# Dynamic time warping on a lane grid: from one direction in 16 segments of 100 rows to both directions in 8 segments of 188 rows

## The reference

```python
def _dtw_cost(D):                    # D: 1500 x 56 distances
    R[i, j] = D[i, j] + min(R[i-1, j], R[i, j-1], R[i-1, j-1])
def _backtrack(R, T1, T2):           # from (1499, 55) back to (0, 0)
    choice = argmin([R[i-1, j-1], R[i-1, j], R[i, j-1]])   # first minimum wins
expanded[j] += context[i]            # for each cell (i, j) of the path
x = x + tanh(g_xattn[0]) * expanded  # tokens are layer-normed before D
```

## Time and profile before

| | |
|---|---|
| median of 3 runs | 528.3 us (528.27 to 529.79) |
| profiled execution | 530.62 us, its span 528.8 us |
| TensorE, VectorE, ScalarE, GpSimd busy | 431.2, 377.7, 262.5, 86.8 us |
| mean granted TensorE clock | 0.948 |

### The profile page before, as it was taken

One profiled execution on the slowest core, in us unless ns is written; L12 is line 12 of the kernel. 1 busy time (PEld: TensorE's weight loads), 2 busy tenths in 40 slices (PEclk: granted clock), 3 DMA queues, 4 the chain that ended last, 5 costly groups with the idle time before them and its releaser, 6 DMA issues.

```text
span 528.8 us, 10186 instructions
## 1 busy us (share of the span) xinstructions
PE 431.2 (82%) x4021; PEld 254.3 (48%) x4021; DVE 377.7 (71%) x995; ACT 262.5 (50%) x454; POOL 86.8 (16%) x101
## 2 busy tenths in 40 slices
PE   9997778758888887101778899999999999989996
PEld 7444333326655573000334456666666666544444
DVE  8668999998666786865685888988979883371112
ACT  4565888655322691100102456666656567634443
POOL 1000000001000005787980000210210211100000
PEclk9999999898999999655798999999999999999999
DMA  8600674325513005963180004384384491000000
GB/s 285 226 0 23 183 213 137 109 89 152 149 58 91 28 2 126 231 150 87 36 175 1 0 1 106 74 176 103 77 177 94 84 285 37 2 1 0 0 1 17
DMA packets 28719, 50.06 MB, mean 95 GB/s; under 512 B 2464, under 2 KB 18400, under 8 KB 28672
## 3 DMA queue, kind: packets, MB, share of 16 engines
q1 hardware_dynamic: 26848, 45.74, 32.3%
q0 software_dynamic: 1536, 3.67, 2.7%
q10 hardware_dynamic: 288, 0.00, 0.0%
HBM read 39.96 MB, written 9.45 MB: 93 GB/s over the span
## 4 chain that ended last, share of the span: by engine, by line
PE 46%; DVE 35%; issue 8%; POOL 7%; ACT 3%; DMA 1%; DVEq 0%; POOLq 0%
PE banks L1626 7%; PE banks L1602 7%; POOL arena L548 6%; PE banks L1657 5%; DVE arena L1230 4%; DVE work L1259 4%; PE banks L1704 4%; DVE mx L1033 4%; PE banks L1718 4%; DVE arena L1283 2%; DVE mx L1041 2%; PE banks L1470 2%; PE banks L1316 2%; DVE work L1225 2%; PE banks L1320 2%
## 5 line engine op out<-in xcount | busy, mean ns | idle before, releaser
L1033 DVE TENSOR_REDUCE mx<-banks 112x1 f32<-112x500 f32 x168 | 106.9, 676 | 18.2 <-PE banks L1602 18.2
L778 ACT ACTIVATE arena<-banks 128x896 f32<-128x896 f32 x96 | 87.9, 917 | 49.9 <-PE banks L1657 49.2
L1340 PE MATMUL banks<-steps,one 128*128 128x500 f16 (+1 forms) x201 | 56.5, 376 | 33.8 <-DVE hcol L981 33.8
L1626 PE MATMUL banks<-arena 128*32 128x112 f32 (+1 forms) x1536 | 58.1, 265 | 3.4 <-issue 2.5
L1602 PE MATMUL banks<-ctxT,arena 128*112 128x500 bf16 x144 | 54.7, 393 | 3.7 <-DVE mx L1041 1.1
L1626 PEld LDWEIGHTS banks<-arena 128*32 128x32 f32 (+1 forms) x1536 | 33.9, 109 | 23.7 <-issue 21.0
L1340 PEld LDWEIGHTS banks<-steps,one 128*128 128x128 f16 x201 | 20.3, 103 | 48.7 <-issue 38.2
L1259 DVE SCALAR_TENSOR_TENSOR work<-twice,banks,arena 128x202 f32<-128x202 f32 x68 | 29.5, 434 | 18.8 <-PE banks L1470 18.8
L1657 PEld LDWEIGHTS banks<-arena,ctxT 128*128 128x128 bf16 (+1 forms) x576 | 37.3, 104 | 9.7 <-issue 1.9
L1657 PE MATMUL banks<-arena,ctxT 128*128 128x112 bf16 (+1 forms) x576 | 40.9, 213 | 0.0
L548 POOL DMA_INDIRECT arena<-in_w_tab,idx x32 | 34.6, 1082 | 11.6 <-issue 9.5
(11 more groups left out here) (264 smaller groups left out, 773.1 us busy)
## 6 DMA issues: line engine op xcount, KB each, us to landing
ctxT<-key_parts SPq DMA_DIRECT2D x36, 375.0 KB, 6.4
key_parts<-arena SPq DMA_DIRECT2D x32, 281.2 KB, 2.9
ctxT<-in_ctx_T SPq DMA_DIRECT2D x12, 500.0 KB, 8.8
arena<-key_parts SPq DMA_DIRECT2D x12, 375.0 KB, 7.9
ctxT<-in_ctx_nat SPq DMA_DIRECT2D x5, 750.0 KB
arena<-in_ctx_nat SPq DMA_DIRECT2D x3, 750.0 KB
arena<-in_L_ffn_W SPq DMA_DIRECT2D x1, 2048.0 KB, 10.0
arena<-in_fold_w SPq DMA_DIRECT2D x1, 768.0 KB, 5.8
```

The lines of the kernel that those rows point to most:

```text
L778: nc.scalar.activation(Pt[0:rows, g % 2, :].rearrange("p (a n) -> p a n", a=2), banks[0:rows, 2 + 2 * (g % 2):4 + 2 * (g % 2), 0:HQ // 2], ...
L1033: nc.vector.tensor_reduce(mx3[:, b % 2, u // NPIECE, u % NPIECE:u % NPIECE + 1], ps[k % 2][0:2 * NJ, 0:PIECE], AX_X, ALU.max).then_inc(s_m ...
L1340: nc.tensor.matmul(bank[:, 0:cols], one16[:, :], steps16[:, 0:cols], start=True, stop=True, skip_group_check=True)
L1626: last = nc.tensor.matmul(ps[6 + b % 2][q:q + 32, o:o + 2 * NJ], vals[0:rows, v0:v0 + 32], Pt[0:rows, g % 2, 2 * t * NJ:2 * (t + 1) * NJ], ...
```

## The change

The recurrence is run from both ends. Batch b has 8 lanes for the forward direction (tokens 0 to 27, rows ascending) and 8 for the backward one (tokens 55 to 28, rows descending). The rows, padded by 2 at each end with a distance of 1e35 to 1504, are cut into 8 segments of 188. So STEPS = 28 + 8 - 1 = 35 and TB = 2, in 18 chunks. There are 16 units of 376 rows of each direction; each unit has four batch-direction streams on 32 columns of the array each, two of them read backwards, and the squares are kept for the whole context. The scan reads the distances directly from PSUM.

Where the two directions meet, the kernel finds the cheapest crossing: GpSimd gathers the last column of each lane (`cross`), TensorE turns the backward one, VectorE adds and finds the minimum and its place, TensorE spreads the start to all lanes. GpSimd also takes the difference of neighbouring jump targets (`growth`), and a hop then sums the differences over the rows that are not above the current one. 34 hops follow, both directions at a time, without filler products. Keys go in 24 pieces of 500 columns. Masks are made for 16 half segments of 94 rows.

```diff
-    LB = P // NB
-    C = 100
-    NS = NI // C
-    STEPS = NJ + NS - 1
+    HJ = NJ // 2
+    NG = 2 * NB
+    LB = P // NG
+    PADU = 2
+    NS = LB
+    C = (NI + 2 * PADU) // NS
+    HC = C // 2
+    NQ = 2 * NS
+    STEPS = HJ + NS - 1
-    TB = 5
+    TB = 2
-    EARLY_VALUES = 16
+    EARLY_VALUES = 8
-    KPIECE = 375
+    KPIECE = 500
-    KEYS_OF_CHUNK = [0, 1] + 7 * [3] + 5 * [2]
+    KEYS_OF_CHUNK = [0, 0, 0] + 4 * [2, 2, 1] + [2, 2, 0]
...
+            def differences(k):
+                t, n = CODES[k]
+                pool.wait_ge(s_carry, k + 1)
+                nc.gpsimd.tensor_tensor(growth[:, t * SLOT1:(t + n) * SLOT1], where[k % 2][:, 1:1 + n * SLOT1],
+                                        where[k % 2][:, 0:n * SLOT1], ALU.subtract).then_inc(s_grow, 1)
+            for k in range(NCODES - 6):
+                differences(k)
+            for s in range(NS - 1):
+                if s % 2:
+                    differences(NCODES - 6 + s // 2)
+                pool.wait_ge(s_scan, HJ + s)
+                nc.gpsimd.tensor_tensor((cross1 if s else cross), view(R, [[1, SLOT]], (HJ + s) * SLOT),
+                                        segment[:, s:s + 1].broadcast_to([P, SLOT]), ALU.mult).then_inc(s_cross, 1)
+                if s:
+                    pool.wait_ge(s_cross, 2 * s)
+                    nc.gpsimd.tensor_tensor(cross, cross, cross1, ALU.add).then_inc(s_cross, 1)
+                    pool.wait_ge(s_cross, 2 * s + 1)
+            for k in range(NCODES - 3, NCODES):
+                differences(k)
...
+                for k in range(2):
+                    last = nc.scalar.activation(
+                        view(dist[:, :], [[NB * BS, 4], [BS, 2], [1, HJ]], 2 * g * BS + (2 * n + k) * JW + PADJ),
+                        view(ps[2 + 4 * (u % 2)][0:HC, :], [[2 * JP, 4], [JP, 2], [1, HJ]], k * 2 * P), ACT.Sqrt)
...
-            D2_AT = {1: (6,), 3: (7,), 5: (8, 9), 7: (10,), 8: (11,)}
+            D2_AT = {1: (6,), 2: (7, 8, 9), 3: (10,), 4: (11, 12, 13), 5: (14,), 6: (15,)}
+            TARGETS_AT = {7: (0,), 9: (1, 2)}
...
-                nc.vector.tensor_tensor_scan(view(R, [[1, C]], (t + 1) * SLOT + 1), m, d,
+                nc.vector.tensor_tensor_scan(view(R, [[1, C]], (t + 1) * SLOT + 1), m,
+                                             ps[t // TB % 2][:, t % TB * C:(t % TB + 1) * C],
...
+            ve.wait_ge(s_scan, STEPS)
+            ve.wait_ge(s_cross, 2 * NS - 3)
+            nc.vector.scalar_tensor_tensor(out=cross, in0=view(R, [[1, SLOT]], STEPS * SLOT),
+                                           scalar=segment[:, NS - 1:NS], in1=cross, op0=ALU.mult, op1=ALU.add
+                                           ).then_inc(s_crossed, 1)
+            jump_inputs(NCODES - 1)
+            rows_not_left(NCODES - 2)
+            ve.wait_ge(s_back, 1)
...
             for t in range(STEPS - 1, 0, -1):
-                if t < STEPS - 1:
-                    ve.wait_ge(s_hop, STEPS - 1 - t)
+                ve.wait_ge(s_hop, STEPS - t)
                 nc.vector.scalar_tensor_tensor(
-                    out=hit_at.rearrange("p (c k) -> p c k", k=2),
-                    in0=twice[:, :].rearrange("p (c k) -> p c k", k=2), scalar=e,
-                    in1=view(where, [[1, SLOT], [0, 2]], t * SLOT),
-                    op0=ALU.is_equal, op1=ALU.mult, accum_out=acc[:, t - 1:t]).then_inc(s_hit, 1)
+                    out=hit_at, in0=twice[:, :], scalar=ps[2][:, t:t + 1],
+                    in1=growth[:, t * SLOT1:(t + 1) * SLOT1],
+                    op0=ALU.is_le, op1=ALU.mult, accum_out=acc[:, t - 1:t]).then_inc(s_hit, 1)
...
-                for h in range(2):
-                    nc.tensor.matmul(ps[4 + u % 2][h * J64:(h + 1) * J64, 0:PIECE], xm2[:, 2 * g + h, :],
-                                     piece(ctxT, u)[:, h, :], start=True, stop=False, skip_group_check=True)
+                for k in range(4):
+                    nc.tensor.matmul(ps[4 + u % 2][k * JP:(k + 1) * JP, lo:hi], xm2[:, g, k // 2, k % 2, :],
+                                     along(ctxT[:, :], u, k), start=True, stop=False, skip_group_check=True)
...
-                keep_busy(ps[3], 1, 384)
```

More of the change, by code:

```diff
@@ L141, in build_gated_layers @@
         R = arena[:, o_R:]
+        M_RING = 2 * TB
+        assert M_RING * C <= 2 * N_B and TB * C <= N_B
         mring = work[:, 0:2 * N_B]
[L144 to L149 removed]
@@ new lines, in build_gated_layers @@
+        rises = [work[:, o_rises + a * HB:o_rises + (a + 1) * HB].bitcast(F16) for a in range(2)]
+        rise = [work[:, (4 + a) * N_B:(5 + a) * N_B] for a in range(2)]
+        left = [work[:, 6 * N_B + a * HB:6 * N_B + (a + 1) * HB].bitcast(F16) for a in range(3)]
+        never = [work[:, 6 * N_B + a * HB:6 * N_B + (a + 1) * HB].bitcast(F16) for a in range(3, 5)]
+        assert 5 * HB <= 2 * N_B
+        back, least, total, place = [work[0:P // 2, o_xn + a * SLOT:o_xn + (a + 1) * SLOT] for a in range(4)]
@@ L152, in build_gated_layers @@
+        WB = TB * SLOT1 // 2 + 1
+        where = [work[:, o:o + WB].bitcast(F16) for o in (M_RING * C, o_xn + 4 * SLOT)]
+        assert M_RING * C + WB <= 2 * N_B and o_xn + 4 * SLOT + WB <= 10 * N_B
+        gate = work[:, 10 * N_B:10 * N_B + TB * SLOT1]
         taken = 0
@@ L192, in build_gated_layers @@
         blk = sb("blk", [P, P])
-        first = sb("first", [P, NB])
+        quarter = sb("quarter", [P, 1])
+        first = sb("first", [P, NG])
+        first3 = first[:, :].rearrange("p (b a) -> p b a", a=2)
+        segment = sb("segment", [P, NS])
+        o_small = 10 * N_B + TB * SLOT1
+        turned = work[:, o_small:o_small + P // 2]
+        o_small += P // 2
+        limit, filled = [work[:, o_small + a * (NF + 1):o_small + (a + 1) * (NF + 1)] for a in range(2)]
+        o_small += 2 * (NF + 1)
+        begin16 = work[:, o_small:o_small + NF // 2].bitcast(F16)
+        o_small += NF // 2
+        nowhere = work[:, o_small:o_small + NF]
+        assert o_small + NF <= 10 * N_B + GATE and NF % 2 == 0
+        lowest = sb("lowest", [P // 2, 1])
+        lowat = sb("lowat", [P // 2, 1])
+        rowmin = sb("rowmin", [1, NB])
+        rowhit = sb("rowhit", [1, P // 2])
+        rowat = sb("rowat", [1, NB])
+        begin = sb("begin", [1, P])
+        zall = sb("zall", [P, STEPS + 1])
         pidx = sb("pidx", [P, 1], I32)
@@ L1270, in _ @@
+            last.then_inc(s_z, 1)
             nc.vector.memset(U, 0.0)
```

504 lines of the change are left out of this document (286 added, 218 removed).

## The result

The changed kernel takes 561.3 us (median of 4 runs, 560.0 to 562.9) against 529.0 for the kernel before in the same comparison: a ratio of 1.0605, 95% interval 1.056 to 1.065. Slower by 6%, where 5% faster was forecast. The profiled execution took 560.8 us, its span is 559.0.

A forecast was written before the change was run, and what follows sets the result against it. It took instruction chains as the bound: TensorE at the start, VectorE in the recurrence, their relay in the hops. Hops ending at 147.3 for 175.46, plus 1.9 behind, gave -26.3: 504.3 profiled, 502 median, range 493 to 513.

The forecast's parts named there:

- The last transfer of context rows: Behind the hops: 770 KB, 6.5 us, starts some 3.5 us ahead of the last hop, covered by masks; uncovered, 3 us.
- the ScalarE term: Recurrence: 15 activations and three signs fill 10.5 of 11.9 us, near the limit; 1 us of stalls, bounds 0 and 4.
- The one on the other side: Rival at the start: quarters don't overlap at all, a unit costs 5.7 us or more, about 560 us; chance 0.03.
- Unit 1.97 us: Start, TensorE: each of 16 units takes 1.97 us with gaps, its products in column quarters overlapping about four-fold.
- Scan 6 at 47.4: End of the start: scan 6 needs the last lane columns and so all 16 units, and comes at 47.4 us.
- Chunk 3.96 us: Recurrence: length of a chunk, against which the loads of ScalarE and GpSimd were reckoned.
- The crossing 8.8 us: Between recurrence and hops: VectorE's operations and waits take 8.8 us, with TensorE's three products covered by the targets.
- Held by GpSimd 4 us: Recurrence: GpSimd slows VectorE, 5 us from differences and 3 in the last seven steps if it exists; 4 taken.
- GpSimd's prices: Recurrence and crossing: a difference of 380 elements takes 0.98 us, a crossing operation of 189 about 0.55.
- Hops 25.0 + 1.5 for the clock: Hops: 34 at 0.735 us, 25.0 us, bounds 23.9 and 29; 1.5 for a clock dip, bounds 0 and 5.
- Behind the hops +1.9: After the hops: placing them +0.45, masks +1.2, last group of sums +0.3; everything later unchanged.
- by that rule 8: Recurrence: by the skill's rule of mutual lockout, GpSimd would cost VectorE 8 us and the time be 506.

The follow-up runs named there:

- the 96-partition kernel: The changed kernel with all eight tiles of context rows on 96 partitions in place of 94, two of zeros: 504.4 us, ratio 0.950 to the kernel before.

## Why the prediction was wrong

**The step that failed** is the last one: "The last transfer of context rows (770 KB, 6.5 us at the 119 GB/s of the hops' stage) starts when value group 21 of 24 is out", and after it "Everything later is as it was." It priced the transfer with the mean rate of a stage of the kernel before, whose tiles had 100 partitions, and looked at the last tile alone. A tile of 94 partitions takes 14.5 us (752 KB at 53.3 GB/s). The six late ones form a chain of 92 us, from 131.8 to 223.8, which is longer than the hops and masks together; the cover of 3.5 us and the masks' 18 is far from enough. This cost 38.0 us. The early tiles weren't in the sum at all: the ScalarE term looked at activations and signs and took 1 us for stalls, without the stores that free its buffers. This cost 19.5 us. Without these two, 504.4 were measured against 502 predicted, and a difference to before of 26.1 us (530.5 to 504.4) against 26.3. That this is so close is in part luck. VectorE began the crossing 2.9 us earlier than forecast (109.1 for 107.0 + 1 + 4), the crossing itself took 10.6 us in place of 8.8, and the hops 27.9 in place of 26.5.

Nor was it among the rivals: every one of them was about instructions of the engines, none about a transfer. The one on the other side (quarters don't overlap, 560) came near the right time by another mechanism; a unit takes 1.97 us and it is refuted.

**Point by point**, read in the 96-partition kernel, predicted value first:
- Unit 1.97 us: 1.97. Four products of 376 columns in quarters take 0.66 us, start to start, about what the forecast's price gives for one of full width (0.68): quarters overlap four-fold, read backwards or not. The row that the forecast drew it from doesn't say so much: 1.6 over 0.59 is 2.7-fold. By that a unit would have been over 0.6 us longer. The choice of four was right without its row.
- Scan 6 at 47.4: 47.3 (46.96 in the changed kernel). Scan 590 ns: 605. Chunk 3.96 us: 3.95; but the sum's own terms give 4.09 (two steps of 1.10, 1.03 and 0.86), so this hit tests none of them.
- ScalarE near its limit: activations of 500 took 0.68 us; no wait of VectorE for codes is left in the trace, so the 1 us of stalls was 0.
- The crossing 8.8 us: 10.6. Its terms as listed add up to 9.2. The trace adds 1.3 us of waiting for the turned column, which the forecast had under cover.
- Held by GpSimd 4 us, bounds 0 and 8: some 3 from the groups' means, and 4.9 with all that hung on it. The cause was put in the wrong place: 5 us of 8 were put down to the differences and 3 to the last seven steps. The differences run beside shuffle and scan and hold next to nothing; the last steps make nearly all of it.
- GpSimd's prices: difference 0.98 predicted, 0.84; a crossing operation 0.55 predicted, 0.61 and 0.67 in the mean, 0.52 where no two-input operation of VectorE ran beside it. The wait 1.5: 1.07.
- First hop 120.8: 119.7.
- Hops 25.0 + 1.5 for the clock, end at 147.3: 27.9, end at 147.6. With the clock held up they took 25.5, so the clock's share was 2.5 and the relay's 0.735 us each right (0.75).
- Behind the hops +1.9: 503.0 - 147.59 = 355.4 against 528.8 - 175.46 = 353.3, +2.1.

The second rule that the prediction drew on, of the Trainium skill (SBUF — State Buffer, section Who interferes with whom), fits the last chunks: 0.53 became 0.85 while GpSimd read SBUF, and GpSimd's sum, 0.52 beside shuffle and scan, took 0.71 there. The "by that rule 8" was my count of meetings, not the page's.

## What to carry to other kernels

When a change alters a tile's number of partitions, price its transfers anew, before any instruction: 100 to 94 partitions, with about the same bytes (750 and 752 KB), cost 57 us, and 95, 96, or a cut into 80 and 14, gave it back. Look in the profile for a DMA share that stays at one level (0.13, 0.30) while the work above it changes; here it was a transfer on few engines. A stage's mean rate is no price for one transfer: the 119 GB/s of the hops were 175 while tiles were in flight. And list what shares the queue with such a transfer: a third of the loss came from stores of other data behind it, through a ring of buffers and three engines' queues.

## What was unexpected of the hardware

- A transfer on two engines holds up transfers that are spread wide: a key store, 2.8 us to landing in the median, took 17.5 us behind a 94-partition tile issued 1.3 us ahead of it.
- One row more (94 to 95) took the rate from 54 to 123 GB/s; per engine it stayed at 25 to 27 GB/s. With more engines each moved less: 175 GB/s at a share of 0.62 and 236 at 0.92 are 18 and 16 GB/s per busy engine.
- Filling TensorE's idle time ahead of the crossing took away one of two falls of the clock, but the other began 6 us earlier and lasted longer (0.50 from 114 to 124 us, where it had been 120 to 126); only when the crossing was filled as well did the clock stay at 2.4 GHz.
